# One fused transformer block on one core: two stationary operands laid out in tiles of 1040 bytes, and thirty unread products at the end

## The reference

```python
h = _layernorm(x) * (1 + ca) + sa
lhs, rhs = h * w_lhs, h * w_rhs
scores = einsum('nsd,ntd->nst', lhs, rhs)          # 1024 x 1024 for each batch
x = x + ga * einsum('nst,ntd->nsd', softmax(scores), h)
h = _layernorm(x) * (1 + cb) + sb
x = x + gb * (relu(h @ W1 + b1) @ W2 + b2)         # 256 -> 1024 -> 256
```

## The kernel before

| products | stationary tile starts every | distance before |
|---|---|---|
| F | 512 bytes (W1hi at 17024, W1lo at 25216; h2hi at 210624, h2lo at 218816) | 64 in all |
| SC | 512 bytes (Lhi at 111680, Llo at 119872; Rhi at 128064, Rlo at 136256) | 0 in all |
| G and GT | 512 bytes (hid_hi at 198336, hid_lo at 204480; W2hi at 33408, W2lo at 41600) | -64 in all |
| AV | 512 bytes (Phi, Plo); V's halves start every 1040 bytes (at 144448) | 0, 16, 32, ... 240 in the course of a step |

## Time and profile before

### The profile page before, as it was taken

One profiled execution on the slowest core, in us unless ns is written; L12 is line 12 of the kernel. 1 busy time (PEld: TensorE's weight loads), 2 busy tenths in 40 slices (PEclk: granted clock), 3 DMA queues, 4 the chain that ended last, 5 costly groups with the idle time before them and its releaser, 6 DMA issues.

```text
span 672.1 us, 13438 instructions
## 1 busy us (share of the span) xinstructions
PE 665.8 (99%) x4481; PEld 612.9 (91%) x4481; DVE 549.5 (82%) x1139; ACT 513.4 (76%) x763; POOL 299.3 (45%) x311
## 2 busy tenths in 40 slices
PE   8999999999999999999999999999999999999998
PEld 8688898998999999999999989999899999999997
DVE  4799879998899789997899898998899977787321
ACT  2367779994899769995899948998599976677463
POOL 3471365155543364523547245352554333625444
PEclk9999999999999999999999999999999999999999
DMA  8141665237732578135662267513773246401300
GB/s 293 55 87 63 196 181 181 80 126 241 184 109 95 137 237 234 47 118 157 189 207 78 94 220 212 130 62 128 254 203 70 96 158 178 140 17 65 101 33 32
DMA packets 76929, 92.27 MB, mean 137 GB/s; under 512 B 9120, under 2 KB 67040, under 8 KB 76896
## 3 DMA queue, kind: packets, MB, share of 16 engines
q1 hardware_dynamic: 76896, 91.85, 45.4%
HBM read 55.33 MB, written 36.50 MB: 137 GB/s over the span
## 4 chain that ended last, share of the span: by engine, by line
PE 97%; DVE 2%; DMA 1%; issue 0%; SPq 0%; ACT 0%; DVEq 0%; ACTq 0%
PE col L675 9%; PE col L674 9%; PE col L673 9%; PE acc L595 8%; PE score L775 8%; PE acc L596 8%; PE acc L601 8%; PE score L771 8%; PE score L772 8%; PE score L663 4%; PE score L662 4%; PE score L664 4%; PE score L764 4%; PE score L636 2%; DMA S<-wmod 1%; PE score L751 1%
## 5 line engine op out<-in xcount | busy, mean ns | idle before, releaser
L1264 POOL TENSOR_TENSOR hid_lo<-hid,hid_hi 128x512 fp32r<-128x512 f32 x127 | 177.6, 1407 | 202.1 <-ACT hid_hi L800 201.7
L796 ACT ACTIVATE hid<-col,b1T 128x512 f32<-128x512 f32 x128 | 87.0, 679 | 69.9 <-PE col L675 65.2
L595 PE MATMUL acc<-W2hi,hid_hi 128*128 128x256 f32 x480 | 117.1, 278 | 0.0
L596 PE MATMUL acc<-W2lo,hid_hi 128*128 128x256 f32 x480 | 116.7, 278 | 0.0
L771 PE MATMUL score<-V,Phi 128*128 128x258 f32 x448 | 108.7, 281 | 0.0
L772 PE MATMUL score<-V,Phi 128*128 128x256 f32 x448 | 108.5, 281 | 0.0
L675 PE MATMUL col<-h2hi,W1lo 128*128 128x512 f32 x256 | 100.9, 394 | 0.0
L674 PE MATMUL col<-h2lo,W1hi 128*128 128x512 f32 x256 | 100.6, 393 | 0.0
L673 PE MATMUL col<-h2hi,W1hi 128*128 128x512 f32 x256 | 100.4, 392 | 0.0
L800 ACT ACTIVATE hid_hi<-hid 128x512 fp32r<-128x512 f32 x128 | 81.0, 633 | 15.3 <-PE acc L601 11.1
L595 PEld LDWEIGHTS acc<-W2hi,hid_hi 128*128 128x128 f32 x480 | 90.3, 188 | 2.5
(11 more groups left out here) (168 smaller groups left out, 1470.5 us busy)
## 6 DMA issues: line engine op xcount, KB each, us to landing
block_rows<-blocks SPq DMA_DIRECT2D x29, 512.0 KB, 2.6
blocks<-block_rows SPq DMA_DIRECT2D x116, 128.0 KB, 2.9
x_cur<-x SPq DMA_DIRECT2D x16, 512.0 KB, 4.1
ln_t<-x SPq DMA_DIRECT2D x14, 512.0 KB, 4.6
score_blocks<-stage SPq DMA_DIRECT2D x14, 512.0 KB, 3.0
S<-score_blocks SPq DMA_DIRECT2D x56, 128.0 KB, 3.6
S<-quarter_blocks SPq DMA_DIRECT2D x56, 96.0 KB, 2.3
out<-x_mlp SPq DMA_DIRECT2D x8, 512.0 KB, 3.6
```

Of the source, the lines that this page charges most:

```text
L595: nc.tensor.matmul(o, hi, W2hi[:, it, :], start=(it == 0 and (apart or t % 2 == 0)), stop=False, skip_group_check=True)
L596: nc.tensor.matmul(o, hi, W2lo[:, it, :], start=False, stop=False, skip_group_check=True)
L796: nc.scalar.activation(hid[:, n % 2, :], col[n % 2][:], ACT.Relu, bias=b1T[:, n % FT:n % FT + 1]).then_inc(col_read, 1)
L1264: G.tensor_tensor(hid_lo[:, n % RING, :], hid[:, n % 2, :], hid_hi[:, n % RING, :].bitcast(F32), ALU.subtract).then_inc(hid_lo_done, 1)
```

## The change

Three things are changed.

1. W1hi, W1lo, Lhi and Llo are laid out by tile: the two 512-byte halves (kk = 0 and 1) of tile i stand side by side, then come 16 unused bytes, so that a tile starts every 1040 bytes and a product's distance falls by 16 bytes from tile to tile. Small tensors and a few unused ones (before_W1lo, before_W2, behind_L_first, before_R) fill the gaps so that the distance of tile 0 stays as it was. F step n now has the distance 64 - 16 (n mod 8), so 64, 48, 32, 16, 0, -16, -32, -48. SC step n has -16 n, so 0 to -112. Inside a step all six or twelve products keep the same distance. W1hi now starts at 17024, W1lo at 25728, Lhi at 112704, Llo at 121408, Rhi at 130112, h2hi at 212672. The other tensors move by 1024 or 2048 bytes, and the distances of G, GT and AV stay as they were, mod 512.
2. ACT, DVE and POOL write and read these four tensors through a pattern with one more dimension; no instruction is added or taken away there, and none moves.
3. Behind the last GT product TensorE makes 30 more products of 256 columns, with h2lo as stationary and h2hi as moving operand, into a PSUM bank that nobody reads. They wait for nothing. They come in six groups of five, with distances of 64, 128, 192, 256, -192 and -128.

```diff
-        W1hi, W1lo = sb("W1hi", [P, DK, FF], F32R), sb("W1lo", [P, DK, FF], F32R)
+        by_tile = lambda rows: rows[:, :, 0:DK * P].rearrange("p i (k c) -> p k i c", k=DK)
+        W1hi = by_tile(sb("W1hi_rows", [P, FT, DK * P + 4], F32R)[:])
+        stats, stats1 = sb("stats", [P, HT, 6]), sb("stats1", [P, HT, 6])
+        mv1, mv2 = sb("mv1", [P, T, 2]), sb("mv2", [P, T, 2])
+        sb("before_W1lo", [P, 16])
+        W1lo = by_tile(sb("W1lo_rows", [P, FT, DK * P + 4], F32R)[:])
...
+        sb("before_W2", [P, 8])
         W2hi, W2lo = sb("W2hi", [P, FT, D], F32R), sb("W2lo", [P, FT, D], F32R)
...
-        Lhi, Llo = sb("Lhi", [P, DK, ROWS], F32R), sb("Llo", [P, DK, ROWS], F32R)
+        Lhi = by_tile(sb("Lhi_rows", [P, T, DK * P + 4], F32R)[:])
...
+        Llo = by_tile(sb("Llo_rows", [P, T, DK * P + 4], F32R)[:])
+        sb("before_R", [P, 96])
         Rhi, Rlo = sb("Rhi", [P, DK, ROWS], F32R), sb("Rlo", [P, DK, ROWS], F32R)
...
-                                nc.tensor.matmul(o, Lhi[:, kk, tile], hi, start=(kk == 0), stop=False)
+                                nc.tensor.matmul(o, Lhi[:, kk, n, :], hi, start=(kk == 0), stop=False)
...
-                            nc.tensor.matmul(col[n % 2][:], W1hi[:, kk, tile], h2hi[:, kk, cols], start=(kk == 0), stop=False)
+                            nc.tensor.matmul(col[n % 2][:], W1hi[:, kk, it, :], h2hi[:, kk, cols], start=(kk == 0), stop=False)
...
+                        for w_at, h_at, count in ((0, 16, 5), (0, 32, 5), (0, 48, 5), (0, 64, 5), (48, 0, 5), (32, 0, 5),):
+                            for _ in range(count):
+                                nc.tensor.matmul(col[0][:, 0:256], h2lo[:, 0, w_at:w_at + P], h2hi[:, 0, h_at:h_at + 256], start=True, stop=True)
...
-                                nc.scalar.activation(Lhi[:, kk, cols], featT[:, kk, :], ACT.Copy, scale=root[:, kk:kk + 1])
+                                tiles = slice(n * HT, (n + 1) * HT)
+                                nc.scalar.activation(Lhi[:, kk, tiles, :], featT[:, kk, :].rearrange("p (t c) -> p t c", c=P), ACT.Copy, scale=root[:, kk:kk + 1])
...
-                                V_.scalar_tensor_tensor(Llo[:, kk, cols], featT[:, kk, :], root[:, kk:kk + 1],
-                                                        Lhi[:, kk, cols].bitcast(F32), ALU.mult, ALU.subtract).then_inc(feat_done, 1)
+                                tiles = slice(n * HT, (n + 1) * HT)
+                                V_.scalar_tensor_tensor(Llo[:, kk, tiles, :], featT[:, kk, :].rearrange("p (t c) -> p t c", c=P), root[:, kk:kk + 1],
+                                                        Lhi[:, kk, tiles, :].bitcast(F32), ALU.mult, ALU.subtract).then_inc(feat_done, 1)
```

More of the change, by code:

```diff
@@ L261, in block_kernel @@
         ident = sb("ident", [P, P])
-        W1hi, W1lo = sb("W1hi", [P, DK, FF], F32R), sb("W1lo", [P, DK, FF], F32R)
+        by_tile = lambda rows: rows[:, :, 0:DK * P].rearrange("p i (k c) -> p k i c", k=DK)
[4 more added lines that the diff above has]
+        W1lo = by_tile(sb("W1lo_rows", [P, FT, DK * P + 4], F32R)[:])
+        row_max, part_max = sb("row_max", [P, T]), sb("part_max", [P, 2, 4, HT])
+        nm1, rs1, nm2, rs2 = sb("nm1", [P, T]), sb("rs1", [P, T]), sb("nm2", [P, T]), sb("rs2", [P, T])
+        var_eps, half_power = sb("var_eps", [P, HT]), sb("half_power", [P, HT])
+        sb("before_W2", [P, 8])
         W2hi, W2lo = sb("W2hi", [P, FT, D], F32R), sb("W2lo", [P, FT, D], F32R)
@@ L289, in block_kernel @@
         Phi, Plo = sb("Phi", [P, RING, T, P], F32R), sb("Plo", [P, RING, T, P], F32R)
-        with nc.sbuf_tensor("L_first", [P, DK, ROWS], F32) as L_first, nc.sbuf_tensor("R_first", [P, DK, ROWS], F32) as R_first:
-            pass
-        Lhi, Llo = sb("Lhi", [P, DK, ROWS], F32R), sb("Llo", [P, DK, ROWS], F32R)
+        with nc.sbuf_tensor("L_first", [P, DK, ROWS], F32) as L_first, nc.sbuf_tensor("behind_L_first", [P, P], F32), \
+                nc.sbuf_tensor("R_first", [P, DK, ROWS], F32) as R_first:
+            pass
+        Lhi = by_tile(sb("Lhi_rows", [P, T, DK * P + 4], F32R)[:])
+        nb1, nb2, inv_sum = sb("nb1", [P, T]), sb("nb2", [P, T]), sb("inv_sum", [P, 1])
+        mod_l, mod_r = sb("mod_l", [P, 2 * DK]), sb("mod_r", [P, 2 * DK])
+        w_sign, w_abs, w_root = sb("w_sign", [P, 2, DK]), sb("w_abs", [P, 2, DK]), sb("w_root", [P, 2, DK])
+        root_power, root, root_r, sign_r = sb("root_power", [P, 2, DK]), sb("root", [P, DK]), sb("root_r", [P, DK]), sb("sign_r", [P, DK])
+        Llo = by_tile(sb("Llo_rows", [P, T, DK * P + 4], F32R)[:])
+        sb("before_R", [P, 96])
         Rhi, Rlo = sb("Rhi", [P, DK, ROWS], F32R), sb("Rlo", [P, DK, ROWS], F32R)
@@ L311, in block_kernel @@
         h2hi, h2lo = sb("h2hi", [P, DK, ROWS], F32R), sb("h2lo", [P, DK, ROWS], F32R)
[L312 to L322, removed]
         wmod_a = S[:, 7, :].rearrange("p (k n) -> p k n", k=DK)
@@ L661, in part @@
                                     hi, lo = Rhi[:, kk, cols], Rlo[:, kk, cols]
-                                nc.tensor.matmul(o, Lhi[:, kk, tile], hi, start=(kk == 0), stop=False)
-                                nc.tensor.matmul(o, Lhi[:, kk, tile], lo, start=False, stop=False)
-                                last = nc.tensor.matmul(o, Llo[:, kk, tile], hi, start=False, stop=(kk == DK - 1))
+                                nc.tensor.matmul(o, Lhi[:, kk, n, :], hi, start=(kk == 0), stop=False)
+                                nc.tensor.matmul(o, Lhi[:, kk, n, :], lo, start=False, stop=False)
+                                last = nc.tensor.matmul(o, Llo[:, kk, n, :], hi, start=False, stop=(kk == DK - 1))
                         last.then_inc(scores_done, 1)
@@ L670, in part @@
                         pe.wait_ge(col_read, NF * f + n + 1)
-                        tile, cols = slice(it * P, (it + 1) * P), slice(half * HR, (half + 1) * HR)
+                        cols = slice(half * HR, (half + 1) * HR)
                         for kk in range(DK):
-                            nc.tensor.matmul(col[n % 2][:], W1hi[:, kk, tile], h2hi[:, kk, cols], start=(kk == 0), stop=False)
-                            nc.tensor.matmul(col[n % 2][:], W1hi[:, kk, tile], h2lo[:, kk, cols], start=False, stop=False)
-                            last = nc.tensor.matmul(col[n % 2][:], W1lo[:, kk, tile], h2hi[:, kk, cols], start=False, stop=(kk == DK - 1))
+                            nc.tensor.matmul(col[n % 2][:], W1hi[:, kk, it, :], h2hi[:, kk, cols], start=(kk == 0), stop=False)
+                            nc.tensor.matmul(col[n % 2][:], W1hi[:, kk, it, :], h2lo[:, kk, cols], start=False, stop=False)
+                            last = nc.tensor.matmul(col[n % 2][:], W1lo[:, kk, it, :], h2hi[:, kk, cols], start=False, stop=(kk == DK - 1))
                         last.then_inc(col_done, 1)
@@ L838, in part @@
                             act.wait_ge(feat_done, DK * ph.turn(b, "TH", n) + kk + 1)
-                            nc.scalar.activation(Rlo[:, kk, cols], Llo[:, kk, cols].bitcast(F32), ACT.Copy, scale=sign_r[:, kk:kk + 1]).then_inc(right_lo, 1)
+                            nc.scalar.activation(Rlo[:, kk, cols].rearrange("p (t c) -> p t c", c=P), Llo[:, kk, n * HT:(n + 1) * HT, :].bitcast(F32), ACT.Copy,
+                                                 scale=sign_r[:, kk:kk + 1]).then_inc(right_lo, 1)
                     elif kind == "WS":
@@ L843, in part @@
                         act.wait_ge(w_in, 32)
-                        nc.scalar.activation(W1hi[:], W1_sb[:], ACT.Copy).then_inc(w_hi_ready, 1)
+                        nc.scalar.activation(W1hi, W1_sb[:].rearrange("p k (i c) -> p k i c", c=P), ACT.Copy).then_inc(w_hi_ready, 1)
                         nc.scalar.activation(W2hi[:], W2_sb[:], ACT.Copy).then_inc(w_hi_ready, 1)
@@ L1291, in part @@
                     elif kind == "WS":
-                        for i, (lo, hi, both) in enumerate(((W1lo, W1hi, W1_sb[:]), (W2lo, W2hi, W2_sb[:]))):
+                        for i, (lo, hi, both) in enumerate(((W1lo, W1hi, W1_sb[:].rearrange("p k (i c) -> p k i c", c=P)), (W2lo, W2hi, W2_sb[:]))):
                             pool.wait_ge(w_hi_ready, i + 1)
```

## The result

The changed kernel takes 676.81 us (median of five runs, 676.38 to 677.71), the kernel before, in five runs beside it, 674.88 us (674.22 to 675.60). The ratio is 1.0032, with a 95% interval of 1.0021 to 1.0042 (it is not the quotient of the two medians). The medians differ by 1.9 us, and the interval stands for 1.4 to 2.8 us. That lies in the predicted range of 671.5 to 681.5 us, 0.7 us above the 676.1 of the forecast. But the forecast had the time rise by 0.6 us, under the 1.35 us that it said can be told from no change, and the rise is clear.

A forecast was written before the change was run, and what follows sets the result against it. TensorE was taken to bound the kernel. Tail +0.4, first layer +0.6 and scores -0.4 gave +0.6 us on the 672.1 us span, 672.7, plus 3.4 for the median: 676.1 us, range 671.5 to 681.5 (8 times in 10).

The forecast's parts named there:

- What bounds the kernel: Whole kernel: TensorE, busy 665.8 of 672.1 us, sets the time by its products' start-to-start costs plus a tail.
- The lines on the other engines: Writes of Lhi, Llo, Rlo and W1hi: priced at 0, hidden by TensorE's work; 3 us if that cover went.
- The tail: Thirty products behind the last GT product: TensorE now arrives last, +0.4 us, bounds 0 to +1.0.
- The first layer: The 128 F steps: half in the cheap, half in the dear state, +0.6 us, bounds -2.7 to +7.3.
- The scores: SC steps: 256-column products gain by leaving distance 0, wider ones nothing; -0.4 us, bounds -2.1 to +2.8.
- Other products: G, GT and AV keep their distances: 0, with 0.8 us either way for G steps opening differently behind F.
- Rival 1: F and SC products: varied distance keeps TensorE unsettled; +6.2 us with the tail, 681.7 us; chance 0.22.
- Rival 2: F and SC: distances 64 and 0 are poor, most others let TensorE settle; -4.4 us, 671.1 us; chance 0.24.
- Rival 3: F and SC: distance has no effect, only the tail remains; +0.4 us, 675.9 us; chance 0.12.
- the 3.4 us around its span: Whole kernel: the runs' median stood 3.4 us above the profiled span of 672.1, and the same was added to the forecast.

The follow-up runs named there:

- side: The changed kernel without the thirty end products, W1 and L in tiles of 1024 bytes so no distance varies; 676.18 us, ratio 1.0003 to before.
- map: The kernel before plus 2048 unread products at its end, at 32 distances in two orders; 256 columns cost 113.3 to 120.0 ns; no whole-kernel ratio given.
- w2_64: The kernel before with W2 alone starting 64 bytes later mod 256, by unused bytes; 682.12 against 675.53 us, ratio 1.0096.
- l_only: The changed kernel without the thirty end products, W1 in tiles of 1024 bytes, so only SC's distance changes; 676.64 us, ratio 1.0013 to before.

## Why the prediction was right or wrong

**What bounds the kernel: right.** TensorE's gaps and the tail moved the time. The lines on the other engines were priced at 0, and side, where ACT, DVE and POOL write and read the four tensors tile by tile as well, is at 1.0003 (0.9993 to 1.0014). What the prediction left out is that TensorE's waits, most of them for Phi and Plo, vary by up to 2.7 us between executions of the same products (1.0 to 3.7 us).

**The tail: right.** +0.4 us forecast, 3.6 to 4.0 us in the trace, 1.0010 (1.0001 to 1.0019) alone. The reason given holds: TensorE's last product ends at 675.68, SyncE's last wait passed at 675.1, and the span ends at 675.9.

**The first layer: little changed, as forecast, but not by the mechanism given.** Forecast +0.6, measured +0.1 in the trace. That the tiles differ and repeat from batch to batch holds. That "an F step is either in the 1.375 state or in the 1.40 state and stays there for all six products" does not: already before, the steps behind SC stand at 1.39 because their first two products take 233 to 237 ns and the later ones 225 to 236, and in the changed kernel steps cost from 1.359 to 1.410 us, 19 of them 1.366 or less. The sum came out small because dearer and cheaper tiles cancel. Mean F step by tile, in us, without the one that held a wait:

| tile | 0 | 1 | 2 | 3 | 4 | 5 | 6 | 7 |
|---|---|---|---|---|---|---|---|---|
| distance | 64 | 48 | 32 | 16 | 0 | -16 | -32 | -48 |
| before | 1.384 | 1.382 | 1.384 | 1.387 | 1.385 | 1.392 | 1.386 | 1.375 |
| changed | 1.379 | 1.391 | 1.394 | 1.375 | 1.373 | 1.380 | 1.389 | 1.400 |

**The scores: wrong in sign, small.** Forecast -0.4, measured +0.3. I took the 256-column products to leave a poor distance; at their new ones they cost 118.9 ns in place of 119.0. The map shows why: 0 is poor for that width, but most others are hardly better. The rise comes from the products of 512 columns, for which I took nothing: 230.9 ns before, 232.3 in the changed kernel, and for that width 0 is the best distance of the map.

**Other products: the step that failed.** The prediction put G, GT and AV at 0, with 0.8 us either way, because they "keep their distances" and only "a G step behind an F step may open a little better or worse". G cost +2.2 us. I had taken what F leaves behind as something that passes in a few products, since in the trace of before it always did. The runs show a second state that lasts as long as the distance does (36 products of 118 ns), met by half of the G runs behind F. In the trace of before G never ended in it, so that trace could not show it; but it did show that an F step at one distance costs 1.375 or 1.40 us by what ran before it, and I used that for F and not for G.

**The rivals.** Rival 1 (varied distance keeps TensorE unsettled) had the sign of the result, but not its place: F and SC together cost 0.4 us more, not 5.8. Rival 2 is refuted where it called 0 a poor distance: for 512 columns it is the best one, 226.7 ns. Rival 3 is refuted by w2_64: it would have stayed at 1.000 and is at 1.0096. The Trainium skill (TensorE: Matmul & The Clock Gate, Step-by-step: what each phase is for) says that the next weight load takes no read bandwidth from the running matmul. That layout is therefore free does not hold in these runs; whether it is the two reads that meet, or something else that goes by the distance of the two operands, no run here shows.

**The time.** 676.1 was 0.7 us low, but the rise was forecast at 0.6 us and is 1.9, and the closeness is partly luck. The forecast started from 675.46 us, and before came to 674.88 beside the changed kernel; that takes 0.6 us off the miss of 1.3. G was missed by 2.2 us, F came 0.5 lower and SC 0.7 higher than forecast: the parts forecast at +0.6 came to +3.0 in the trace, and the medians show less than that, probably because the waits shrank. The start was off as well, without harm: the profile of before was one of few waits and the 3.4 us around its span should have been 1.8, two errors that cancel, since the 3.4 was the median less that span.

## What to carry to other kernels

Where TensorE bounds a kernel of float32r products of 256 to 512 columns, start addresses mod 256 are a tuning knob that costs a few unused bytes; here single layouts ran from 0.3% faster to 1.0% slower than before. But their effect depends on the order of steps too: a layout can't be judged by the step whose operands it moves, since the state goes on into the next steps. Read gaps from start to start, product by product, and look for a repeated pattern: two patterns for one distance are a state, and the cause stands ahead of it. A replay of the product sequence at the end of the kernel prices dozens of layouts in one run; here it agreed with two batches of the kernel to within 1 ns on every product.

## What the runs showed of the hardware

- Float32r products with a new weight load each: 113.3 ns is the lowest steady gap for 256 columns and 226.7 ns for 512, at a granted clock of 1.0. Those are 1.06 times 256 and 512 cycles of 2.4 GHz (106.7 and 213.3 ns).
- The price depends on the distance of moving operand and next stationary operand with a period of 256 bytes in steps of 16 (the finest tried): 113.3 to 120.0 ns, and 226.7 to 236.7 ns.
- At distances 16 and 192 there are two steady states for 256 columns (113.3 and 119.0, 113.3 and 117.8 ns), chosen by what ran before; at 32 there are two as well (117.8 and 120.0). The dear one at 192 held for all of 36 products, and by l_only what a step leaves can reach through an F step in between.
- Neither other engines' work nor the output's bank changed a gap by over 1 ns in the two batches of before that agree with the replay throughout. Why the states exist is open: no run here separates the reads of the two operands in time.
